# Six routing pieces of the last 15 token tiles moved from attention's steps 4 to 9 into steps 4 to 6

## The reference

```python
x = x + attn(layernorm(x))       # rows 0..15 of each batch attend; every other row gets only the bias ob
h = layernorm(x)
scores = sigmoid(h @ router.T)   # 32 experts in 4 groups of 8
# by scores + bias: the 2 best groups (sum of their 2 best), in them the 4 best experts
w = scores[chosen] / sum(scores[chosen]) * 2.5
mixed = sum_k w_k * down_k(silu(gate_k(h)) * up_k(h))
out = x + mixed + shared_expert(h)
```

## Time and profile before

| what | value |
|---|---|
| median of 3 runs | 532.5 us (531.38 to 534.62) |
| profiled execution, its own time | 529.38 us |
| its span | 527.6 us |
| PE / PEld busy | 384.5 us (73%) / 296.1 us (56%) |
| DVE busy | 268.6 us (51%) |
| ACT busy | 235.4 us (45%) |
| POOL busy | 295.1 us (56%) |
| DMA | 100.94 MB, mean 191 GB/s |

### The profile page before, as it was taken

How to read it: one execution, slowest core, us unless ns; L and a number is a source line. 1 busy time by engine, 2 the same in 40 slices (tenths; PEclk the granted TensorE clock), 3 DMA queues, 4 the chain that set the end, 5 groups by cost and what they waited for, 6 DMA issues and landing times.

```text
span 527.6 us, 8705 instructions
## 1 busy us (share of the span) xinstructions
PE 384.5 (73%) x1930; PEld 296.1 (56%) x1930; DVE 268.6 (51%) x977; ACT 235.4 (45%) x604; POOL 295.1 (56%) x435
## 2 busy tenths in 40 slices
PE   0678997958775787119999999999999999900000
PEld 0677855525443454018888888888888888700000
DVE  3888177996660436303666322222233332319997
ACT  0586743372543743204555555555555555500000
POOL 4624885888888884612556666666555556620000
PEclk9999998997996999758999999999999999965555
DMA  7941232224999989665545554455455545259996
GB/s 178 263 205 42 100 107 75 102 100 145 246 249 257 249 326 350 249 204 155 149 141 175 164 155 147 147 173 150 153 170 152 164 134 171 81 187 407 380 404 248
DMA packets 45734, 100.94 MB, mean 191 GB/s; under 512 B 8553, under 2 KB 26606, under 8 KB 44144
## 3 DMA queue, kind: packets, MB, share of 16 engines
q1 hardware_dynamic: 32672, 66.66, 40.6%
q0 software_dynamic: 12720, 33.64, 19.2%
q10 hardware_dynamic: 288, 0.03, 0.0%
HBM read 53.93 MB, written 47.55 MB: 192 GB/s over the span
## 4 chain that ended last, share of the span: by engine, by line
PE 47%; POOL 19%; DMA 11%; DVE 9%; issue 8%; ACT 3%; SPq 1%; POOLq 0%; DVEq 0%; ACTq 0%
PE two_banks L923 23%; POOL slots_dram L535 15%; PE two_banks L940 11%; DVE x_sb L1450 7%; DMA slots_dram<-loopb,slot_i 6%; PE two_banks L909 6%; DMA gu_w<-pairs_dram 3%; PE two_banks L929 3%; POOL pause L538 2%; PE two_banks L795 2%; POOL rstd L482 2%; DMA x_sb<-in_x 1%; ACT loopb L599 1%; PE two_banks L770 1%; DVE stats L1017 1%
## 5 line engine op out<-in xcount | busy, mean ns | idle before, releaser
L542 POOL DMA_INDIRECT pairs_dram<-routing,loopb x137 | 134.8, 984 | 103.5 <-issue 82.7
L535 POOL DMA_INDIRECT slots_dram<-loopb,slot_i x128 | 127.6, 997 | 51.4 <-issue 22.6
L923 PE MATMUL two_banks<-gu_w,routing 128*128 x548 | 142.9, 384 | 0.1
L1421 DVE TENSOR_TENSOR routing<-routing,two_banks 128x128 f32<-128x128 f32 x137 | 39.4, 287 | 160.5 <-ACT routing L687 147.7
L923 PEld LDWEIGHTS two_banks<-gu_w,routing 128*128 128x128 f32 x548 | 94.7, 193 | 7.9 <-issue 0.5
L682 ACT ACTIVATE routing<-two_banks 128x256 f32<-128x256 f32 x137 | 52.6, 384 | 85.9 <-PE two_banks L909 84.8
L940 PE MATMUL two_banks<-dn_w,routing 128*128 x274 | 81.8, 381 | 0.0
L909 PE MATMUL two_banks<-ident,loopb 128*128 128x128 f32 x274 | 53.2, 277 | 22.4 <-DMA loopb<-slots_dram 22.4
L770 PE MATMUL two_banks<-gu_w,sgu_w 128*128 128x512 f32 x128 | 62.9, 629 | 0.4 <-ACT loopb L610 0.4
L909 PEld LDWEIGHTS two_banks<-ident,loopb 128*128 128x128 f32 x274 | 39.0, 143 | 36.6 <-DMA loopb<-slots_dram 22.7
L1450 DVE SCALAR_TENSOR_TENSOR x_sb<-gu_w,wts,x_sb 128x256 f32<-128x256 f32 x128 | 51.0, 480 | 11.8 <-DMA gu_w<-pairs_dram 11.8
(11 more groups left out here) (234 smaller groups left out, 387.1 us busy)
## 6 DMA issues: line engine op xcount, KB each, us to landing
loopb<-slots_dram SPq DMA_DIRECT2D x137, 128.5 KB, 2.2
gu_w<-pairs_dram SPq DMA_DIRECT2D x32, 512.0 KB, 7.8
slots_dram<-gu_w SPq DMA_DIRECT2D x32, 257.0 KB, 15.4
gu_w<-in_gate_up SPq DMA_DIRECT2D x4, 2048.0 KB, 11.8
out<-x_sb SPq DMA_DIRECT2D x3, 1024.0 KB
dn_w<-in_down SPq DMA_DIRECT2D x1, 2304.0 KB, 15.9
pairs_dram<-routing,loopb POOLq DMA_INDIRECT x137, 2.6
x_sb<-in_x SPq DMA_DIRECT2D x2, 1024.0 KB, 13.4
```

The source lines that it names most:

```text
L535: pool.indirect_dma_start(out=slots_dram, out_offset=bass.IndirectOffsetOnAxis(ap=slot_i[:, at:at + 1], axis=0), in_=xg[:, r, 0:ROW], in_o ...
L542: pool.indirect_dma_start(out=pairs_dram, out_offset=bass.IndirectOffsetOnAxis(ap=xg[:, u % RING, D:ROW].bitcast(I32), axis=0), in_=yb[u % ...
L923: ins = pe.matmul(bank[2 + u % 2][:, 0:2 * I], xT[:, u % 2, c, :], w, start=(c == 0), stop=(c == KC - 1))
```

## The change

The table that says which routing piece is done in which step of attention is changed for part 2; the same seven pieces stand in steps 4 to 6 in place of 4 to 9.

```diff
 ROUTE_AT = {0: [(1, 0), (1, 1)], 1: [(1, 2), (1, 3)], 2: [(1, 4)], 3: [(1, 5), (1, 6)],
-            4: [(2, 0)], 5: [(2, 1)], 6: [(2, 2)], 7: [(2, 3)], 8: [(2, 4)], 9: [(2, 5), (2, 6)]}
+            4: [(2, 0), (2, 1), (2, 2)], 5: [(2, 3), (2, 4)], 6: [(2, 5), (2, 6)]}
 RANK_AT = {step + 1: part for step, pieces in ROUTE_AT.items() for part, piece in pieces if piece == 4}
```

## The result

The changed kernel takes 539.6 us (538.3 to 540.8, 5 runs) where the kernel before takes 534.6 (531.4 to 535.3, 5 runs): ratio 1.011, 95% interval 1.007 to 1.015. In this and every later measurement the ratio and its interval leave out executions that were over 1.5% above the fastest of the same kernel, while medians and ranges in us are of all executions. It is slower, as forecast, by 5.0 us where 14.7 were forecast; 539.6 lies just under the range of 540 to 553. The two profiled executions lie further apart: 540.5 (span 538.7) against 529.4 (span 527.6), 11.1 us. So there are two things to explain: 3.6 us of 14.7 that the trace itself does not show, and the 6 us between the traces' difference and that of the medians.

What follows compares the result with a forecast made beforehand. Up to 233 us, scatters, their landing and ScalarE's staging were taken to bound the kernel. Terms from 98.04 put the softmax at 125.8; GpSimd, staging and end each +14.7, so 532.5 + 14.7 = 547.2 us, range 540 to 553.

Steps and rivals of the forecast that it cites:

- Step 4 to step 6, the ranks: VectorE's moved pieces and TensorE's rank matmuls ahead of L854: a 14.6 us stop, 1.87 us of matmuls, softmax 18.2 later.
- the clock: TensorE behind its long stop: half clock for 4.1 us, costing 1.1; "up" matmuls end at 121.4, bounds 120.1 and 124.
- GpSimd's holes: GpSimd waits for late stage(12) and stage(13): a hole of 5.4 us, then that tile starts 14.7 us late.
- Attention 10 late: After the late softmax, attention gains some back: L871 at about 133.1 where it was 122.74, about 10 us late.
- "If a landing takes as long as it did, each follows GpSimd": stage(20) to stage(23), waiting for the tile four before, each come 14.7 us later, with landings of 8.6 us.
- its term for the blank rows: Blank-row writes from 124.2: 1.95 MB alone, 6.5 MB at 146 GB/s beside scatters, landed by about 177 instead of 186.
- The claim that stage(23) decides: ScalarE's stage(23) moves from 161.74 to 176.4; a chain with almost no holes from there carries 14.7 us to the end.
- rival 1: Scatter landings get short and attention's lateness decides: +6 to +10 us, say 541; chance 0.11.
- "On that scale 532.5 + 14.7": End of the sum: profiled execution lies 3.1 us under the median, so the loss is added to 532.5, giving 547.2.
- 2 (the loss grows by the load on top of the ring): Second GpSimd hole, second half-clock stretch, weight load from 177 on stage(27)'s landing: +18 to +22, say 552; chance 0.09.
- rival 3: Faster: ranks don't hold L854, blanks start some 20 us sooner, stage(23) doesn't wait, 5 to 8 us go: 526; chance 0.03.
- 4: The change does nothing that counts: stagings catch up in GpSimd's 9.79 us of slack, 532.5; chance 0.05.

Runs made afterwards that it cites:

- the early stagings: Changed kernel with stage(12), (13) and (14) all in attention's step 5, ahead of ScalarE's copy that waits for L854: 537.1 us, ratio 1.014.
- the later ranks: Changed kernel with part 2's rank matmuls one step later, behind L854 and ahead of L860: 538.6 us, ratio 1.017.
- the second and third measurements: Later timings beside the kernel before (529.2 and 528.6 us); the unedited changed kernel was timed only in the earlier one: 544.9 us, ratio 1.027.
- load held: Changed kernel with SP's load of the first expert weights held until ScalarE has staged tile n=29: 538.6 us, ratio 1.011.
- blanks held: Changed kernel with the 32 blank-row writes held until ScalarE has staged tile n=16: 544.5 us, ratio 1.029.
- product first: Changed kernel with (2,1) and (2,2) in step 5, behind the product L1316 and ahead of (2,3) and (2,4): 543.3 us, ratio 1.027.
- the fourth and fifth measurements: Later timings on one chip: kernel before 533.1 and 532.5 us; the unedited changed kernel, timed only in the earlier one, 537.7 us, ratio 1.011.
- the kernel with both edits: Changed kernel with rank matmuls one step later and stage(12) to (14) in step 5: 539.8 us, ratio 1.021.
- The candidate: Changed kernel with rank matmuls a step later, stage(13) to (15) in step 6, and the weight load held until n=29 is staged: 529.7 us, ratio 1.001.

## Why the prediction was wrong in size

*Step 4 to step 6, the ranks, the clock.* Right, term by term: the stop 14.69 for 14.6, the ranks' matmuls to L854 1.76 for 1.87, L860 at 120.16 for 120.2 (121.4 less 1.16), the softmax 124.64 for 124.6. The lower clock behind the stop lasted at least 4.3 us, and the value taken near the lower bound was good.

*GpSimd's holes.* 6.21 and 8.62 us where 5.4 and 9.3 were forecast; GpSimd then ran 14.2 us behind the earlier trace rows. Right, and shown to matter by the early stagings (-7.9 us) and the later ranks (-6.4 us). Attention 10 late: L871 at 131.92 is 9.2 behind, 10.3 with the earlier start.

*"If a landing takes as long as it did, each follows GpSimd".* This is the first step that failed, by its term for the blank rows. I gave them 8.5 us alone at 230 GB/s, the pace at which SP had issued them beside scatters, and 250 GB/s for blanks and scatters together. Measured, all DMA moved 291 GB/s from 124 to 132 us, with no scatter issued, and 267 from 133 to 165, beside scatters:

```profile
133.00:165.00 32.00, 24.87 (x119) 14.20 (x115) 12.93 (x32) 15.63 (x27) 27.34 (x50) 0.89 1.05 267
```

So the blank rows were gone by 171 in place of 177, and tile n=19's last scatter, issued at 167.58, had landed by 172.07, in 4.5 us or less for 8.6. stage(23) came 3.2 us sooner than forecast. For attention alone that makes 14.7 - 1.2 (the earlier start) - 3.2 = 10.3 us; the trace has 11.1, since GpSimd, still 15.1 us late, set stage(29). The claim that stage(23) decides failed with it: in this trace it did not. That is rival 1 in part, which I had given 0.11.

In the second and third measurements the rate from 133 to 165 us was 236 and 237 GB/s, the blank rows landed at 182.10 and 178.27, stage(23) came at 178.47 and 177.02 (176.4 forecast), and the loss was 15.7 and 14.8 us: there the sum was right. Over the six traces of the changed kernel and its near variants (load held, blanks held, product first), tile n=19's last scatter took at most 4.5 to 5.5 us where the blank rows were gone by 171, and 9.5 to 10.0 us where they lasted to 178 or, held, to 200. The prediction had room for 250 GB/s only; with 267 stage(23) came at 172, with 236 at 177 to 178.

The prediction also left out a wait that its own row shows: the 8.62 us of the earlier trace rows are the landing for which stage(24) waited (3.05 us, before), not stage(23).

*"On that scale 532.5 + 14.7".* The second and larger miss, 6 us: I laid the loss on the median as if it were the profiled execution moved by 3 us. That failed too. On the chip of the fourth and fifth measurements, whose medians are like the first result's, the kernel before is spread over 9 to 13 us, with its profiled execution, 529.0, near the low end, as the first trace of before, 529.4, lies under the range timed with the first result. Holding the weight load takes the upper part away (527.1, 524.9 to 528.9). So the kernel before there pays 4 to 5 us for a load that starts too soon, by the waits most likely in its meeting with tile n=25's scatters; and the changed kernel does not pay: its load starts at 171, its stage(29) waits for GpSimd's pace in any case, and holding the load changed nothing. With the load held in both, on that chip, the two are 538.6 and 527.1: the change loses 11.5 us (10 by the ratios), as its trace has it, and without the hold gets some 5 of it back. That the first result was of this kind is argued from its medians (534.6 and 539.6, beside 533.1 and 537.7), not shown: there is no trace of an execution of the kernel before at 533 or more. That 539.6 came within a microsecond of the range is therefore luck: two effects that the sum did not have, on both sides of the comparison, took 10 us off it.

*Rivals.* 2 (the loss grows by the load on top of the ring) had the right collision in the wrong kernel: it was seen in the kernel with both edits and in the kernel before. 3 and 4 did not happen. The candidate, with L854 no longer held by the ranks, was level with the kernel before, so even with the blanks out 11 us sooner (rival 3 had 20) there was no gain, which speaks against rival 3's 5 to 8 us.

*Open.* Why blanks and scatters together move at 267 GB/s on one chip and at 236 on others, so that the blank rows land 7 to 11 us apart; and whether the kernel before is at 529 on those others because its load starts later there. No trace of the kernel before was taken on them.

## What to carry to other kernels

When work is moved up on one engine, look for what is released by its last piece on another: here TensorE stood 14.7 us in place of 6.4, for three rank matmuls that stand ahead of the next step's transposes. A load that starts "when its memory is free" starts at a time which another transfer sets; if it can fall on transfers that a small ring waits for, tie it to the ring instead: one wait was worth 4 to 5 us and much of the spread on the one chip where it was tried alone. And before a loss from one trace is laid on a median, ask whether that trace is of the median's kind; where a kernel's runs are spread wider than its trace explains, look for a wait that the trace hardly shows.

## What was not expected of the hardware

The same program differs by measurement in how fast mixed transfers move: the 32 writes of 257 KB of the changed kernel were issued in 28.8 to 29.1 us with the first result and in the fourth measurement, and in 32.5 to 33.1 us in the second and (with the product first) the third, behind the same start; alone, before the scatters came, they moved at 290 to 310 GB/s on all of these chips (from 124.6 to 130 us). A scatter's landing, 2.7 us alone, was mostly 8 to 10 us wherever a large transfer ran beside it, blanks or weights, and fell back when these were over. By the Trainium skill (DMA: Bandwidth & Descriptors, Queues, rings and completion order) a DMA engine takes turns between the queues that have work, packet by packet. If that is what makes a scatter slow, it is slow as long as the other queue has anything; the traces agree (in the changed kernel the median landing is 8.9 us for those issued at 142 to 156, 6.2 at 164 to 168, the last few microseconds of the blank rows, and 2.7 at 184 to 198).
